# A routed mixture-of-experts kernel: experts picked by MAX and MAX_INDEX per group, router weights behind the shared steps, one-hot tiles as narrow operations

## The reference, cut to what matters

```python
probs = jax.nn.softmax(x @ W_router)            # E = 8 (L1, L3) or 16 (L2) experts
top_v, top_i = jax.lax.top_k(probs, 2)          # two experts per token
routed = sum over the two: top_v * expert[top_i](x)
shared = down(act(up(x)))                       # L1, L3: silu(gate) * up; L2: gelu
x = x + 0.5 * (routed + shared)                 # L3: shared * sigmoid(x @ W_sgate)
```

## Time and profile before

| | before |
|---|---|
| time, median of 3 runs | 3247.46 us (3237.97 to 3249.4) |
| profiled execution, first to last instruction | 3310.2 us |
| mean granted TensorE clock of that execution | 0.924 |
| PE busy | 2869.5 us (87%) |
| DVE busy | 2213.8 us (67%) |
| POOL busy | 1556.3 us (47%) |
| ACT busy | 1489.4 us (45%) |

### The profile page before, as it was taken

The page is one execution under the profiler, slowest core; times in us unless marked ns, Lnnn a source line. Parts: engine busy times, 40 slices in busy tenths (PEclk is TensorE's granted clock), DMA queues, the critical chain, the costliest instruction groups (busy, mean ns, idle before and its releaser), DMA issues. The chain is left out here.

```text
span 3310.2 us, 60075 instructions
## 1 busy us (share of the span) xinstructions
PE 2869.5 (87%) x20922; PEld 2560.7 (77%) x20922; DVE 2213.8 (67%) x5794; ACT 1489.4 (45%) x3235; POOL 1556.3 (47%) x1511
## 2 busy tenths in 40 slices
PE   8979999999999899886897967579997858977798
PEld 6869999999999787774686947557776746956697
DVE  6767777777777677765636656478886555654655
ACT  3356565666566524335323443345444334433342
POOL 2345556555555216444401346658882547350143
PEclk9989999999999898997899977879997869988899
DMA  4022122212121302361005434600003442550533
GB/s 149 1 74 68 53 71 55 71 55 71 55 71 55 114 1 79 103 223 34 20 0 191 122 96 151 205 8 2 2 2 140 118 128 81 193 185 1 204 104 98
DMA packets 147763, 285.78 MB, mean 86 GB/s; under 512 B 20673, under 2 KB 70209, under 8 KB 144385
## 3 DMA queue, kind: packets, MB, share of 16 engines
q1 hardware_dynamic: 113458, 211.38, 19.3%
q0 software_dynamic: 21216, 57.96, 6.6%
q10 hardware_dynamic: 12816, 12.78, 1.1%
HBM read 191.59 MB, written 90.45 MB: 85 GB/s over the span
## 5 line engine op out<-in xcount | busy, mean ns | idle before, releaser
L1724 POOL DMA_INDIRECT MXG<-dxn,IDX x250 | 237.3, 949 | 233.9 <-PE bank L1281 174.3
L1736 POOL DMA_INDIRECT YG<-dyo,POSI x192 | 187.6, 977 | 212.7 <-DMA dyo<-YS 107.7
L2688 POOL TENSOR_SCALAR SX<-SX,MN 128x256 f32<-128x256 f32 x256 | 233.7, 929 | 46.0 <-DVE MN L2619 45.9
L1573 POOL TENSOR_TENSOR SHL<-SGS,SHH 128x512 fp32r<-128x512 f32 x36 | 49.0, 1362 | 425.0 <-ACT SHH L1375 422.8
L2619 DVE CUSTOM_DVE_ANT_0 SX<-bank,FMASK 128x128 f32<-128x128 f32 (+1 forms) x512 | 156.1, 351 | 48.1 <-PE bank L2532 48.0
L1098 POOL TENSOR_TENSOR HL<-HID,HH 128x512 fp32r<-128x512 f32 x56 | 72.4, 1292 | 241.7 <-ACT HH L1063 241.5
L546 PE MATMUL bank<-MWH,GH 128*128 x500 | 171.9, 344 | 13.2 <-DVE HB L1644 6.6
L1411 ACT ACTIVATE GH<-bank 128x256 fp32r<-128x256 f32 x250 | 96.5, 387 | 179.5 <-PE bank L1281 173.6
L546 PE MATMUL bank<-MWH,SHH 128*128 128x256 f32 x352 | 111.7, 317 | 73.6 <-POOL SHL L1573 26.5
L548 PE MATMUL bank<-MWH,GL 128*128 x500 | 156.1, 312 | 0.0
L547 PE MATMUL bank<-MWL,GH 128*128 x500 | 156.0, 312 | 0.0
(11 more groups left out here) (465 smaller groups left out, 11634.0 us busy)
## 6 DMA issues: line engine op xcount, KB each, us to landing
dyo<-YS SPq DMA_DIRECT2D x250, 128.0 KB
RAW<-in_wheads SPq DMA_DIRECT2D x68, 320.0 KB
BB<-dgates SPq DMA_DIRECT2D x68, 256.0 KB, 3.6
GB<-dgates SPq DMA_DIRECT2D x68, 256.0 KB, 4.2
RAW<-in_eL SPq DMA_DIRECT2D x32, 304.0 KB
dkeptL<-MWL SPq DMA_DIRECT2D x32, 304.0 KB
dkeptL<-MWH SPq DMA_DIRECT2D x32, 304.0 KB
MWH<-dkeptL SPq DMA_DIRECT2D x8, 1216.0 KB, 13.3
```

What stands on the lines that cost most here:

```text
L1724: nc.gpsimd.indirect_dma_start(MXG[:, n % XGS, :], None, dxn, bass.IndirectOffsetOnAxis(ap=IDX[:, b:b + 1], axis=0)).then_inc(x_in[n % XGS ...
L1736: nc.gpsimd.indirect_dma_start(YG[:, i % YGS, :], None, dyo[0:m.blocks * P, :], bass.IndirectOffsetOnAxis(ap=POSI[:, c * NT + t:c * NT + t ...
L2688: nc.gpsimd.tensor_scalar(part, part, MN[:, n % RING2, 1:2], None, ALU.subtract).then_inc(s_less1, 1)
```

## The change

- **Picking.** `moe_tops` works per group of four tiles as that group's logits come in: four `MAX` (eight largest of each token), one subtraction of the largest, four `MAX_INDEX`. The groups' logits alternate between two PSUM banks, so `logits_sum` of groups 2 and 3 waits for `moe_tops` of groups 0 and 1. `moe_picks` makes both one-hot picks in one `is_equal`, then `MB`. `moe_best`, `moe_shift`, `moe_first` and `moe_second` are gone.
- **Weights.** `Exp` on ACT and the sum, reciprocal and product on DVE move behind all early shared steps. L3's shared gate is copied to SBUF and its sigmoid taken from there.
- **One-hots.** A chunk is 16 `TENSOR_SCALAR` operations: eight of 128x48 with two per-partition scalars and eight of 128x128 with one, instead of three wide `TENSOR_TENSOR`. `BLF`, `LOF` and `IDF`, the scalars, are fp32.
- **Order.** The prefix sums stand behind up 0 instead of up 2; places and slots in step 0; chunks 0 and 1 in step 1; 2 and 3 in step 2; index and experts in step 3. On PE inverses 0 and 1 stand behind up 2 and inverses 2 and 3 behind up 3, each ahead of the down of the step before. POOL makes the low parts of steps 2 and 3 only, DVE all others.

The diff's core:

```diff
@@ logits_sum (PE)
+            g = p // 2
+            if st.kind == 'moe' and p % 2 == 0 and g >= 2:
+                pe.wait_ge(r_tops, GROUPS * st.moe + g - 1)
+            o = bank[LOGITS[g % 2] if st.kind == 'moe' else LOGIT]
@@ moe_tensor (PE)
-                if s == 2:
+                if s == 0:
                     moe_prefix(pe, st)
-                if s == 4:
-                    moe_inverse(pe, st, 0)
-                if s == 5:
-                    moe_inverse(pe, st, 1)
-                if s in (6, 7):
-                    moe_inverse(pe, st, s - 4)
+                if s in (2, 3):
+                    moe_inverse(pe, st, 2 * s - 4)
+                    moe_inverse(pe, st, 2 * s - 3)
                 if s:
                     shared_down(pe, st, s - 1)
-            if m.early == 6:
-                moe_inverse(pe, st, 2)
             shared_down(pe, st, m.early - 1)
-            if m.early == 6:
-                moe_inverse(pe, st, 3)
@@ moe_scalar (ACT), behind the loop over the early steps
+            act.wait_ge(routed, 4 * st.moe + 2)
+            nc.scalar.activation(ME[:, :, 0:m.E], ML1[:, :, 0:m.E], ACT.Exp)
+            nc.scalar.activation(TE[:, :, :], TD[:, :, :], ACT.Exp).then_inc(r_exp, 1)
@@ new on DVE
+        def moe_tops(dve, st, g):
+            dve.wait_ge(r_logits, HALF * st.rt + 2 * g + 2)
+            for t in tiles:
+                last = nc.vector.max(TOP[:, t, :], o[:, t, 0:E])
+            step(last)
+            nc.vector.tensor_tensor(ML1[:, part, 0:E], o[:, part, 0:E], TOP[:, part, 0:1].to_broadcast([P, GROUP, E]), ALU.subtract)
...
+            for t in tiles:
+                last = nc.vector.max_index(TOPI[:, t, :], TOP[:, t, :], o[:, t, 0:E])
+            last.then_inc(r_tops, 1)
@@ moe_hot (DVE)
-            step(nc.vector.tensor_tensor(HOT[:, :, :], BLH[:, cols].unsqueeze(2).to_broadcast([P, CHUNK, NBP]),
-                                         IOH[:, 0:NBP].unsqueeze(1).to_broadcast([P, CHUNK, NBP]), ALU.is_equal))
-            step(nc.vector.tensor_tensor(AHOT[:, c % 2, :, :], HOT[:, :, :],
-                                         IDH[:, tiles].unsqueeze(2).to_broadcast([P, CHUNK, NBP]), ALU.mult))
-            nc.vector.tensor_tensor(BHOT[:, c % 2, :, :], LOH[:, cols].unsqueeze(2).to_broadcast([P, CHUNK, P]),
-                                    IOH[:, :].unsqueeze(1).to_broadcast([P, CHUNK, P]), ALU.is_equal).then_inc(r_hot, 1)
+            for i in range(CHUNK):
+                n = c * CHUNK + i
+                nc.vector.tensor_scalar(AHOT[:, c % 2, i, :], IOH[:, 0:NBP], BLF[:, n:n + 1], IDF[:, n % NT:n % NT + 1], ALU.is_equal, ALU.mult)
+            for i in range(CHUNK):
+                n = c * CHUNK + i
+                last = nc.vector.tensor_scalar(BHOT[:, c % 2, i, :], IOH[:, :], LOF[:, n:n + 1], None, ALU.is_equal)
+            last.then_inc(r_hot, 1)
@@ shared_low, moe_pool: which engine makes the low parts
-                if s < LOWS_BY_VECTOR:
+                if s < LOWS_BY_VECTOR or s >= LOWS_BY_VECTOR + 2:
                     shared_low(dve, nc.vector, st, s)
```

More of the change, by code:

```diff
@@ L8 @@
 I32 = mybir.dt.int32
+U16 = mybir.dt.uint16
 F16 = mybir.dt.float16
@@ L167, in size_of @@
         def size_of(shape, dt):
-            n = 2 if dt in (BF16, F16) else 4
+            n = 2 if dt in (BF16, F16, U16) else 4
             for s in shape[1:]:
@@ L208, in build @@
         IOH = main.put('IOH', [P, P], F16)
-        IDH = main.put('IDH', [P, NT], F16)
+        IDF = main.put('IDF', [P, NT])
         M128 = main.put('M128', [P, NT])
@@ L1396, in moe_scalar @@
                 pieces_high(act, st, 0, min(m.J, 4))
[L1397 to L1402, removed]
+            if st.name == 'L3':
+                act.wait_ge(r_tops, GROUPS * (st.moe + 1))
+                nc.scalar.activation(SGT[:, :], SGT[:, :], ACT.Sigmoid)
             act.wait_ge(xn_out, 16 * GROUPS * (st.moe + 1))
@@ L1459, in moe_scalar @@
                     ahead2_scalar(act, ahead2_slot(m, k))
-        def moe_best(st, which):
-            E = st.m.E
[L1465 to L1474, removed]
@@ L1494, in moe_second @@
-        def moe_second(dve, st):
-            E = st.m.E
-            step(nc.vector.scalar_tensor_tensor(MT[:, :, 0:E], MM[:, 0, :, 0:E], -4.0, ME[:, :, 0:E], ALU.mult, ALU.add))
-            moe_best(st, 1)
-            nc.vector.tensor_tensor(MB[:, 0:E, :].rearrange('p e t -> p t e'), MM[:, 0, :, 0:E], MM[:, 1, :, 0:E], ALU.add).then_inc(routed, 1)
+        def moe_tops(dve, st, g):
+            tiles, part = tiles_of(g)
+            E, o = st.m.E, bank[LOGITS[g % 2]][:, 0:256].rearrange('p (t e) -> p t e', e=16)
+            dve.wait_ge(r_logits, HALF * st.rt + 2 * g + 2)
[3 more added lines that the diff above has]
+            nc.vector.tensor_tensor(ML1[:, part, 0:E], o[:, part, 0:E], TOP[:, part, 0:1].to_broadcast([P, GROUP, E]), ALU.subtract)
+            if st.name == 'L3':
+                nc.vector.tensor_copy(SGT[:, part], o[:, part, E])
+            for t in tiles:
+                last = nc.vector.max_index(TOPI[:, t, :], TOP[:, t, :], o[:, t, 0:E])
+            last.then_inc(r_tops, 1)
@@ L1609, in moe_vector @@
                 front_vector(dve, st)
-            moe_shift(dve, st)
-            moe_first(dve, st)
+            for g in range(0 if st.tailed else GROUPS):
+                moe_tops(dve, st, g)
+            moe_picks(dve, st)
+            moe_gaps(dve, st)
             for s in range(m.early):
                 shared_product(dve, st, s)
-                if s < LOWS_BY_VECTOR:
+                if s < LOWS_BY_VECTOR or s >= LOWS_BY_VECTOR + 2:
                     shared_low(dve, nc.vector, st, s)
+                if s == 0 and st.name == 'L3':
+                    nc.vector.tensor_scalar(SGT[:, :], SGT[:, :], 0.5, None, ALU.mult)
+                if s == 0:
+                    moe_places(dve, st)
+                    moe_slots(dve, st)
+                if s == 1:
+                    moe_hot(dve, st, 0)
+                    moe_hot(dve, st, 1)
+                if s == 2:
+                    moe_hot(dve, st, 2)
                 if s % m.J == 0 and s:
                     shared_add(dve, st, s // m.J - 1)
-                if s == 0:
-                    moe_second(dve, st)
-                if s == 1:
-                    moe_places(dve, st)
                 if s == 2:
-                    moe_slots(dve, st)
-                    moe_hot(dve, st, 0)
+                    moe_hot(dve, st, 3)
                 if s == 3:
-                    moe_hot(dve, st, 1)
+                    moe_index(dve, st)
                     moe_experts(dve, st)
-                if s == 4:
-                    moe_hot(dve, st, 2)
-                if s == 5:
-                    moe_hot(dve, st, 3)
-                if s == (5 if m.early == 6 else 7):
-                    moe_index(dve, st)
             shared_add(dve, st, m.pre - 1)
+            moe_weights(dve, st)
             def low(b):
@@ L1669, in moe_vector @@
             nx = st.next
-            for k in range(m.front_of(GROUPS - 1) + (3 if nx else 1)):
+            for k in range(m.front_of(GROUPS - 1) + (5 if nx else 1)):
                 tiles = [t for t in range(NT) if k == m.slot_of(t)]
@@ L1692, in moe_vector @@
                         front_moments(dve, nx, g)
+                for g in range(GROUPS if nx and nx.kind == 'moe' else 0):
+                    if k == m.front_of(g) + 4:
+                        moe_tops(dve, nx, g)
                 if nx and nx.kind == 'attn2':
```

75 lines of the change are left out of this document (39 added, 36 removed).

## The result

The changed kernel takes 3269.39 us (3268.61 to 3272.23, 4 runs) against 3242.72 us for the kernel before, measured beside it (3234.76 to 3249.4): ratio **1.0081**, 95% interval 1.0068 to 1.0094. It is slower by 26.7 us.

What follows compares the result with a forecast made beforehand. Path alternates between DVE and PE in stages 1 to 4; late steps in 5 and 6 are PE alone. Stage sums give +17.9 us, less 2.4 for the walk running long: +15.5, 3263 us, range 3226 to 3293.

Steps and rivals of the forecast that it cites:

- The new order: Main term: PE waits for chunks before the inverses, later steps queue behind; +4.1 us for stages 1 and 2.
- The third wait: PE in stage 2, behind up 3: a wait of 2.3 us for chunk 3.
- the walk: Step-by-step timing of DVE and PE from T0, the first shared matmul; stage 4 ends at 35.3 against 34.31, +1.
- The chunk's price: One chunk of 16 narrow DVE operations takes 2.65 us, bounds 1.4 and 3.55.
- 24 us per us: Chunk price moves chunk 3 by four times the difference, in six stages: 24 us per us.
- POOL's port: Rival: DVE operations wait until POOL's end, one or two more per chunk in stages 1, 3, 5; 3278 us, chance 0.10.
- The front: Ahead of T0, a logits group takes 2.7 instead of 2.1 us; +1.2 us in stages 1, 2, 4, 6.
- The ends: At the windows' ends: no first-turn wait -1.25 us, first blocks find tokens -0.8, table load about +0.7.
- the turn's wait: First turn's wait for its gather behind the warm matmuls; it goes because the index is early, -1.25 us.
- Picking: Softmax and two rounds go: 7 us won on the routing's path, none yet on PE's; `MB` at T0 + 2.5.

Runs made afterwards that it cites:

- experiments 1 to 4: The kernel before, unchanged, run beside the first four groups of follow-up kernels: median 3243.3 us.
- Experiment 3: Changed kernel with inverses 0 and 1 behind up 3 and inverses 2 and 3 behind up 4 on PE, one step later: 3262.87 us.
- 4: Changed kernel with the three wide one-hot operations of before instead of 16 narrow ones, in the new order: 3249.16 us, ratio to before 1.0018.
- experiment 10: Kernel before with new picking and late weights, logits in banks by halves, experts behind the index; old order, wide one-hots: 3226.79 us, ratio 0.9949.
- experiment 2: Changed kernel with logits of groups 0 and 1 in one bank, 2 and 3 in the other, so PE never waits for picking: 3263.17 us.
- experiment 11: Changed kernel with logits in banks by halves, wide one-hots, one chunk per step, and later inverses, index and experts: 3228.19 us, ratio to before 0.995.
- experiment 6: Changed kernel with the low parts of steps 2 and 3 also on DVE instead of POOL: 3264.37 us.
- 9: Changed kernel with eight matmuls whose result nobody reads ahead of each of two waits for picking, in stages 1, 2, 4, 6: 3264.7 us.
- second execution of before: The kernel before, unchanged, profiled once more: span 3242.2 us, time 3244.95 us.

## Why the prediction came out as it did

The direction and the main mechanism were right, and several sizes were not: +15.5 us were forecast, +26.7 measured beside the kernel before (+26.1 against the larger sample of experiments 1 to 4, 3269.39 - 3243.31).

- *The new order* (+4.1 in stages 1 and 2, more PE time behind the chunks): the mechanism was right. In stage 2 `MB` came at T0 + 2.5 and PE's first two waits at the inverses took 4.8 and 2.4 us, as walked; the last chunk came at T0 + 28.0 instead of 25.9, of which 1.3 us are up 0 at the low clock; four dearer chunks explain the rest. The third wait did not come, and the low clock behind the first two, which took its place, was not forecast. In stage 4 the walk was short: its window grew by 6.3 us instead of 1, with PE 7.5, 2.4 and 3.5 us idle before the inverses. Experiment 3 shows that PE's queue is a cause, and 4 with 10 put a size on the order, low parts included: with the same picking and the same one-hots the new order stands 22 us above the old (25 if each is taken against the kernel before beside it), of which experiment 2 gives about 6 to the banks; 16 to 19 remain. Experiments 3 and 11 agree: 6.5 for the later inverses and 10.7 for one chunk per step.
- *The chunk's price* was mis-sized: 2.65 taken, 2.92 measured. The row with one scalar gave 0.165 for 128 columns, and 0.163 was measured; the second scalar, for which "may cost more" stood, adds some 0.06 to each of eight operations (0.202 measured against the forecast's estimate of 0.145). At the forecast's own 24 us per us this is +6.5. By the Trainium skill, VectorE: DVE Perf Modes, section on the TRN2 errata, the two would take 0.094 and 0.073, an estimate from its figures. The measurement decides against these figures, and for the section's advice against many small tiles: wide one-hots are 20 us faster.
- *POOL's port*, a rival with 0.10, was in part the truth, in stages 3 and 5: three chunks of 7.1 to 7.2 us, 12.5 us above three undisturbed ones of 3.0. It named "one or two" POOL operations per chunk; a run of narrow operations met four, all that POOL had. Not all of it reached the time: experiment 6 took 14.3 us from the chunks and 5 from the time. By the Trainium skill (SBUF — State Buffer, section Who interferes with whom) the port is locked for a whole instruction. The 5.79 us for 1.70 beside 4.96 us of POOL agree with that.
- *The front* (+1.2 in four stages): the wait for picking came in stages 2 and 6 (0.7 and 0.8 us); in stage 4 there was none, and in stage 1 0.4 us that ended on ACT. `moe_tops` took 1.1 us a group instead of 1.4. The low clock at T0 was not forecast. Experiments 2 and 9 set the front at 5 to 6 us, against the 4.8 forecast. That the sum came out near is luck.
- *The ends*: the turn's wait of 1.25 us went, as said, in stages 1, 2 and 4. Stage 4's loop gained up to 6.5 us from early gathers at full clock, which was not forecast; it cancels the window's miss, so that stage 4's +1.3 for +0.9 is luck. Stage 3, with +7.1 for +1.0, missed most: its gathers came 3.5 us later, behind PE's waits.
- *Picking*: "none yet on PE's" path was wrong. With the late weights, in the old order, it is worth 16 to 20 us (experiment 10). In the changed kernel the narrow form, the places and the banks lose twice that: experiment 11, which mends these three and keeps the picking, stands 41 us lower.

What stays open: how much of stage 3's loop is the wait for tokens and how much the clock, and why the clock at T0 is low in some executions and high in others (stage 2 of the kernel before: 246 ns in one execution, 454 in the other).

## What to carry to other kernels

An operand made earlier helps only where its reader's in-order queue has nothing ready behind the wait: put the reader where the operand is already there, even if the result then comes later. Before splitting a wide operation, price the split by a row with the same kind of operands, each scalar counted, and count what runs on POOL beside it: each POOL operation can hold one piece. Count a long wait on PE twice where the clock is seen to fall behind it. And look for the part of a change that wins alone; here it was hidden under three that lost.

## What the runs showed of the hardware

- A pause of 0.72 us on PE in an otherwise dense stretch was followed by the low clock (0.61 over the next 5 us); in the run with eight matmuls without use in its place, 1.05 us, the clock there was 1.00, and 4.7 us were saved in all. A pause of 0.71 us in another run was followed by 1.00, and in the second execution of before the clock fell with no pause.
- Behind PE's waits of 4.8 and 2.4 us the clock was 0.50 for 6 us, and matmuls that take 4.3 us at 1.00 took 6.9.
- Beside four POOL operations, 4.96 us long, eight narrow DVE operations took 5.79 us instead of 1.70.
- `MAX_INDEX` is two instructions, and both are short; in stage 2 of the kernel after, on DVE:

```profile
1763.15 0.08 DVE L1478 MATCH_VALUE_LOAD TOPI<-TOP,bank 128x8 f32 x1
1763.22 0.17 DVE L1478 FIND_INDEX8 TOPI<-TOP,bank 128x8 uint16<-128x8 f32 x1
```

- A `TENSOR_SCALAR` with two per-partition scalars has a longer pitch on 48 columns (0.202 us) than one with a single scalar on 128 (0.163 us).
